# First cross attention on one core: scores of two chunks together, the second score pass on two row halves, key weights folded, tokens rounded on ScalarE

## What is computed

```python
xn = _ln(x, lnx_g, lnx_b)
yn = _ln(y, lny_g, lny_b)            # y: the context, 1500 tokens of 64 features
q = jnp.einsum('bsc,hcd->bhsd', xn, wq)
k = jnp.einsum('btc,hcd->bhtd', yn, wk)
v = jnp.einsum('btc,hcd->bhtd', yn, wv)
a = jax.nn.softmax(jnp.einsum('bhsd,bhtd->bhst', q, k) * D ** (-0.5), axis=-1)
o = jnp.einsum('bhst,bhtd->bhsd', a, v)
```

## Time and profile before

| | |
|---|---|
| median of 3 runs | 628.56 us (625.13 to 633.34) |
| profiled execution | 629.66 us, span 627.8 us, mean granted clock 0.98 |
| busy in the span | PE 566.9 us, PEld 416.1, DVE 444.7, ACT 372.0, POOL 380.6 |
| score matmuls L1143 | first at 115.9 us, last at 304.9 us |
| batch 3 of the first cross attention | 189.98 to 214.50 us |

### The profile page before, as it was taken

How to read it: one execution, slowest core, us unless ns; L and a number is a source line. 1 busy time by engine, 2 the same in 40 slices (tenths; PEclk the granted TensorE clock), 3 DMA queues, 4 the chain that set the end, 5 groups by cost and what they waited for, 6 DMA issues and landing times.

```text
span 627.8 us, 18969 instructions
## 1 busy us (share of the span) xinstructions
PE 566.9 (90%) x8256; PEld 416.1 (66%) x8256; DVE 444.7 (71%) x698; ACT 372.0 (59%) x623; POOL 380.6 (61%) x271
## 2 busy tenths in 40 slices
PE   9788898899999999999888979977889889889897
PEld 4566775566767767666777556664667767778765
DVE  3876728697887887786356774776888988986543
ACT  2335674657657667566462417474677777777552
POOL 1572451488989889864630231175999999977500
PEclk9789999999999999999999999997999999999998
DMA  5830015002101101010013000412422432330000
GB/s 169 238 133 2 3 40 180 2 1 42 34 7 41 26 15 40 3 40 3 2 60 123 2 0 3 99 39 64 103 67 45 96 78 52 78 77 4 2 1 15
DMA packets 33838, 31.81 MB, mean 51 GB/s; under 512 B 27124, under 2 KB 27380, under 8 KB 33756
## 3 DMA queue, kind: packets, MB, share of 16 engines
q1 hardware_dynamic: 33756, 30.60, 18.8%
HBM read 13.06 MB, written 0.23 MB: 21 GB/s over the span
## 4 chain that ended last, share of the span: by engine, by line
PE 62%; DVE 18%; ACT 8%; issue 7%; POOL 3%; DMA 1%; DVEq 0%; POOLq 0%; ACTq 0%
PE psum L1143 9%; DVE scratch L1306 6%; PE psum L1067 5%; PE psum L1119 5%; PE psum L1503 4%; PE psum L1112 4%; PE psum L1114 4%; PE psum L1526 4%; DVE scratch L1291 4%; PE psum L217 3%; POOL scratch L1291 2%; ACT scratch L1276 2%; POOL scratch L652 1%; PE psum L1073 1%; PE psum L248 1%
## 5 line engine op out<-in xcount | busy, mean ns | idle before, releaser
L1291 POOL TENSOR_TENSOR scratch<-scratch 125x896 bf16<-125x896 f32 x143 | 242.7, 1715 | 80.4 <-ACT scratch L1276 79.9
L1306 DVE TENSOR_REDUCE scratch<-psum 128x1 f32<-128x500 f32 x336 | 210.3, 672 | 23.1 <-PE psum L1067 9.6
L1276 ACT ACTIVATE scratch<-psum 125x896 f32<-125x896 f32 x192 | 173.6, 917 | 82.8 <-PE psum L1143 51.1
L1112 PE MATMUL psum<-tok_high,scratch 125*128 125x65 bf16 x1344 | 107.0, 194 | 3.3 <-issue 2.7
L1114 PE MATMUL psum<-tok,scratch 125*128 125x64 bf16 x1344 | 106.4, 194 | 0.0
L1112 PEld LDWEIGHTS psum<-tok_high,scratch 125*128 125x128 bf16 x1344 | 94.8, 98 | 13.9 <-ACT scratch L1276 6.0
L1114 PEld LDWEIGHTS psum<-tok,scratch 125*128 125x128 bf16 x1344 | 88.6, 98 | 17.1 <-issue 0.5
L1143 PE MATMUL psum<-scratch 65*128 65x448 bf16 (+1 forms) x384 | 87.3, 352 | 0.0
L1291 DVE TENSOR_TENSOR scratch<-scratch 125x896 bf16<-125x896 f32 x49 | 67.5, 1383 | 22.8 <-ACT scratch L1276 21.1
L1119 PE MATMUL psum<-tok_high,scratch 125*128 125x65 bf16 x1344 | 72.7, 194 | 4.8 <-POOL scratch L1291 3.1
L1503 PE MATMUL psum<-scratch 128*128 128x500 bf16 x168 | 64.2, 382 | 10.8 <-DVE scratch L1306 6.5
(11 more groups left out here) (340 smaller groups left out, 870.5 us busy)
## 6 DMA issues: line engine op xcount, KB each, us to landing
nrm<-scratch SPq DMA_DIRECT2D x64, 96.0 KB, 2.2
nrm<-w_third SPq DMA_DIRECT2D x32, 96.0 KB, 2.2
raw<-ctx_dram SPq DMA_DIRECT2D x4, 672.0 KB
w_third<-fifth_dram SPq DMA_DIRECT2D x3, 595.0 KB, 6.0
w_third<-third_dram SPq DMA_DIRECT2D x2, 844.0 KB, 8.9
w_third<-third_dram SPq DMA_DIRECT2D x2, 843.5 KB, 6.8
w_fourth<-fourth_dram SPq DMA_DIRECT2D x3, 542.5 KB, 5.8
scratch<-scratch SPq DMA_DIRECT2D x8, 192.0 KB, 2.6
```

The costliest lines, as they stand in the source:

```text
L1112: nc.tensor.matmul(psum[:, sums, 65 * r:65 * r + 65], rows, t1[:, c, :], start=(c == 0 and r == 0), stop=False, skip_group_check=True)
L1276: nc.scalar.activation(CR["p"][0:CP, n % RING, :].rearrange("p (f n) -> p f n", f=2), psum[0:CP, S:S + 2, 0:HALF], ACT.Exp).then_inc(self. ...
L1291: ops.tensor_tensor(CR["pl"][0:CP, n % RING, :], CR["p"][0:CP, n % RING, :], p_high(n % RING), ALU.subtract).then_inc(done, 1)
L1306: nc.vector.tensor_reduce(mxp[:, r, t:t + 1], bank(B, TB), X_AXIS, ALU.max).then_inc(self.aux_freed, 1)
```

## The change

- **Key weights.** `fold_keys_pool`: the first column of a head's key weights is subtracted from the other 63 and from itself. The normalized features of a token add up to zero, so the first feature's term moves into the others and its row is no longer needed. The front waits for this before Q.
- **Second pass.** The first feature's row becomes the row of ones and the shift. `yb` has this row and the 63 others twice, in rows 0 to 63 and 64 to 127; of `qb`, the first half of the columns stands in rows 0 to 63 and the second half in rows 64 to 127. So the two matmuls of the second pass have 64 rows each, in different row halves, and write different banks. The ones are four memsets, the copies into `yb` are two DMAs, and the shift units make 448 columns each (eight matmuls, not seven).
- **Two chunks together.** For even n, `scores_pe` issues the first pass of n and of n+1, then the second pass of n and of n+1; for odd n nothing. The first pass of n+1 waits for the exponential of n-1.
- **Tokens.** GpSimd scales both halves of batch b+2 in chunk 1 and takes the rest in chunk 11; the rounding is done by ScalarE in chunks 4 and 5 (`high_tokens`). Before batch 2, all three steps stay on GpSimd (`split_tokens`).

The core of the diff, with one line of context at most:

```diff
         y_ones = sem("y_ones")
+        ONES = 1.0 + 16256.0 / 2 ** 23
+        def fold_keys_pool(pool):
+            keys = par("a2_wk").rearrange("p (h d) -> p h d", d=65)
+            nc.gpsimd.tensor_copy(keys[:, :, 64:65], keys[:, :, 0:1]).then_inc(key_scaled, 1)
+            pool.wait_ge(key_scaled, 2)
+            nc.gpsimd.tensor_tensor(keys[:, :, 0:64], keys[:, :, 0:64], keys[:, :, 64:65].to_broadcast([128, HEADS, CD]),
+                                    ALU.subtract).then_inc(key_scaled, 1)
+            pool.wait_ge(key_scaled, 3)
             for i in range(2):
-                nc.gpsimd.memset(CR["yb", i][64:65, :], 1.0).then_inc(y_ones, 1)
-                pool.wait_ge(y_ones, i + 1)
+                for k in range(2):
+                    nc.gpsimd.memset(CR["yb", i][64 * k:64 * k + 1, :].bitcast(F32), ONES).then_inc(y_ones, 1)
+                    pool.wait_ge(y_ones, 2 * i + k + 1)
...
                         if b < 3:
-                            pe.wait_ge(y_ones, 2)
+                            pe.wait_ge(y_ones, 4)
                         pe.wait_ge(self.max_set, b + 1)
-                    for r in range(4 * k, min(4 * k + 4, ROWT)):
-                        mm = nc.tensor.matmul(psum[:, B, 128 * (r % 4):128 * (r % 4) + 128],
-                                              nmx[:, r:r + 1].to_broadcast([128, 128]), ident16[:, :],
-                                              start=True, stop=True)
+                    for r in range(3 * k, 3 * k + 4):
+                        lo, hi = max(128 * r, HALF * k), min(128 * r + 128, HALF * k + HALF)
+                        mm = nc.tensor.matmul(psum[:, B, lo - HALF * k:hi - HALF * k],
+                                              nmx[:, r:r + 1].to_broadcast([128, 128]),
+                                              ident16[:, lo - 128 * r:hi - 128 * r], start=True, stop=True)
...
                 pe.wait_ge(act_done.sem, act_done.count("qa"))
-                pe.wait_ge(key_scaled, 1)
+                pe.wait_ge(key_scaled, 3)
...
             def scores_pe(self, pe, n):
-                b, c, i = n // CHUNKS, n % CHUNKS, n // CHUNKS % 2
-                S = 2 + 2 * (n % 2)
-                for lhs, rhs, rows in ((CR["ya", i], CR["qa", i], 128), (CR["yb", i], CR["qb", i], 65)):
-                    if c == 0 and rows != 128:
-                        self.wait_freed(pe, self.index("A", 1, b))
-                        pe.wait_ge(self.yb_in, 16 * (b + 1))
-                        pe.wait_ge(self.front_low, 2)
+                if n % 2:
+                    return
+                b, i = n // CHUNKS, n // CHUNKS % 2
+                chunk = lambda m: slice(128 * (m % CHUNKS), 128 * (m % CHUNKS) + 128)
+                if n == 0:
+                    self.wait_freed(pe, self.index("A", 1, 0))
+                for m in (n, n + 1):
+                    if m >= 2:
+                        pe.wait_ge(self.probs, m - 1)
                     for f in range(2):
-                        mm = nc.tensor.matmul(bank(S + f, HALF), lhs[0:rows, 128 * c:128 * c + 128],
-                                              rhs[0:rows, HALF * f:HALF * f + HALF],
-                                              start=(rows == 128), stop=(rows != 128), skip_group_check=True)
-                return mm
+                        nc.tensor.matmul(bank(2 + 2 * (m % 2) + f, HALF), CR["ya", i][:, chunk(m)],
+                                         CR["qa", i][:, HALF * f:HALF * f + HALF], start=True, stop=False,
+                                         skip_group_check=True)
+                if n % CHUNKS == 0:
+                    self.wait_freed(pe, self.index("A", 1, b))
+                    pe.wait_ge(self.yb_in, 32 * (b + 1))
+                    pe.wait_ge(self.front_low, 2)
+                for m in (n, n + 1):
+                    for f in range(2):
+                        rows = slice(64 * f, 64 * f + 64)
+                        mm = nc.tensor.matmul(bank(2 + 2 * (m % 2) + f, HALF), CR["yb", i][rows, chunk(m)],
+                                              CR["qb", i][rows, HALF * f:HALF * f + HALF], start=False, stop=True,
+                                              skip_group_check=True)
+                        if f:
+                            mm.then_inc(self.scores, 1)
...
                         sums_of_earlier()
-                    if n >= 2:
-                        pe.wait_ge(self.probs, n - 1)
-                    if n < 2:
-                        self.wait_freed(pe, self.index("A", 1, 0))
-                    mm = self.scores_pe(pe, n)
-                    mm.then_inc(self.scores, 1)
+                    self.scores_pe(pe, n)
...
                 if kind == "A":
-                    tile, row = self.shift_row(i)
+                    if b and self is cross1:
+                        self.wait_freed(act, self.index("Q", 1, b))
+                    lo, hi = HALF * k, HALF * k + HALF
+                    tile, row = self.shift_row(i, k)
...
                     self.high_act(act, b + 2, 0)
+                if c in (4, 5) and b < BATCH - 2:
+                    self.high_tokens(act, b + 2, c - 4)
...
                     cols = slice(HALF * k, HALF * k + HALF)
-                    nc.vector.tensor_tensor(CR["qb", i][0:64, cols], bank(B, HALF, 64), CR["qa", i][0:64, cols],
-                                            ALU.subtract).then_inc(self.aux_freed, 1)
+                    nc.vector.tensor_tensor(CR["qb", i][64 * k:64 * k + 64, cols], bank(B, HALF, 64),
+                                            CR["qa", i][0:64, cols], ALU.subtract).then_inc(self.aux_freed, 1)
...
                     projected()
+            def scale_tokens(self, pool, b, k):
+                at = slice(CHUNKS * b + 6 * k, CHUNKS * b + 6 * k + 6)
+                nc.gpsimd.tensor_tensor(nrm[:, at, :], nrm[:, at, :], bc(crstd[:, at], CD), ALU.mult
+                                        ).then_inc(tok_scaled, 1)
                 if self is cross1:
-                    nc.gpsimd.tensor_tensor(src, src, bc(crstd[:, at], CD), ALU.mult).then_inc(tok_scaled, 1)
+                    self.scale_tokens(pool, b, k)
                 nc.gpsimd.tensor_copy(tok[i][:, lot, 64:128], src).then_inc(self.tok_high, 1)
+                self.low_tokens(pool, b, k)
+            def high_tokens(self, act, b, k):
+                at = slice(CHUNKS * b + 6 * k, CHUNKS * b + 6 * k + 6)
+                act.wait_ge(self.pv_done, CHUNKS * (b - 2))
+                if self is cross1:
+                    act.wait_ge(tok_scaled, 2 * b + k + 1)
+                nc.scalar.activation(tok[b % TOKENS][:, 6 * k:6 * k + 6, 64:128], self.src[:, at, :], ACT.Copy
+                                     ).then_inc(self.tok_high, 1)
+            def low_tokens(self, pool, b, k):
+                i, lot = b % TOKENS, slice(6 * k, 6 * k + 6)
                 pool.wait_ge(self.tok_high, 2 * b + k + 1)
-                nc.gpsimd.tensor_tensor(tok[i][:, lot, 0:64], src, tok[i][:, lot, 64:128],
-                                        ALU.subtract).then_inc(self.tok_set, 1)
+                nc.gpsimd.tensor_tensor(tok[i][:, lot, 0:64], self.src[:, CHUNKS * b + 6 * k:CHUNKS * b + 6 * k + 6, :],
+                                        tok[i][:, lot, 64:128], ALU.subtract).then_inc(self.tok_set, 1)
                         self.low_part(pool, nc.gpsimd, n, self.low_pool)
-                    if c in self.split_at and b < BATCH - 2:
-                        if b:
-                            pool.wait_ge(self.pv_done, CHUNKS * b)
-                        if self is cross1 and b == 2:
-                            pool.wait_ge(cx_rstd, 2)
-                        self.split_tokens(pool, b + 2, self.split_at.index(c))
+                    if b < BATCH - 2:
+                        self.tokens_pool(pool, b, c)
+            def tokens_pool(self, pool, b, c):
+                if c == 1:
+                    if b == 2:
+                        pool.wait_ge(cx_rstd, 2)
+                    for k in range(2):
+                        self.scale_tokens(pool, b + 2, k)
+                if c == CHUNKS - 1:
+                    for k in range(2):
+                        self.low_tokens(pool, b + 2, k)
...
                 sp.wait_ge(self.ya_in, 16 * (b + 1))
-                sp.dma_start(CR["yb", b % 2][0:64, :], CR["ya", b % 2][64:128, :]).then_inc(self.yb_in, 16)
+                if b:
+                    sp.wait_ge(self.yb_in, 32 * b)
+                for k in range(2):
+                    sp.dma_start(CR["yb", b % 2][64 * k + 1:64 * k + 64, :], CR["ya", b % 2][65:128, :]
+                                 ).then_inc(self.yb_in, 16)
...
             y_ones_set(pool)
+            fold_keys_pool(pool)
```

26 lines of the change are left out of this document (16 added, 10 removed).

## The result

The changed kernel takes 635.22 us (median of 20 runs, 630.57 to 637.42), the kernel before 630.31 us (median of 20, 624.88 to 633.34), all on the same occasion. The ratio is 1.0077 with a 95% interval of 1.0052 to 1.0102: slower by 4.9 us, between 3.3 and 6.4, well inside 2%. The forecast was 630.5 with a range of 620 to 636.5 and "within 2%" as the likeliest case, so both held, but the step was sized at +2.2 us. Of the 4.7 us between 630.5 and 635.22, 1.8 come from the base: the kernel before has its median at 628.56 in three runs and at 630.31 in twenty. The profiled execution took 636.18 us (span 634.4).

The account below looks back on a forecast made before the run. TensorE was taken as the bound, busy 90% of the span. Seven batches at +0.43 us (+3.0) and the last at -0.8 gave +2.2 us, a median near 630.8; forecast 630.5 us, range 620 to 636.5.

Parts of the forecast that it names:

- parts 1 and 2: Scores of a chunk pair: overlapping row halves save 0.38 us, height changes cost 0.21, giving 1.36 us against 1.52.
- (a): Rival, faster: the drain is cheap for long matmuls, a pair costs 1.15 us, whole near 622.5; chance 15%.
- (b): Rival, slower: row halves do not run beside each other, a pair costs 1.74 us, whole 648; chance 4%.
- part 3: First half of a batch: chunk 5's first pass waits 0.64 us, the output product loses 0.29; net +0.10 us.
- parts 4 and 5: Second half of a batch: steady pairs gain 0.30 us, but 0.97 us stand before the shift rows; net +0.33.
- Rival (c): Forecast waits at chunks 4 and 11 are a third of a microsecond too long each; whole near 626, chance 15%.
- part 6: Work off the path: GpSimd's 1.8 us a batch is worth nothing; key transfers issue far ahead of use.
- Seven batches with next maxima: 7 x 0.43: Seven of the first cross attention's eight batches each grow by 0.43 us, together +3.0 us.
- the forecast case: Whole kernel: the walk through the batches holds, median 627 to 634 us; chance 60%.
- the 6% for trouble of ScalarE at chunks 4 and 5: Case: an exponential queues behind a late cast on ScalarE, TensorE behind it; 634 to 645 us, chance 6%.
- The last ... -0.8 us: Last batch, without next maxima: three pairs give 0.5 us and the end 0.3, so -0.8 us.
- The fold ... in the same group: Front: GpSimd's fold is ready between 88.0 and 90.8 us, before Q at 93.37; without that cover 2.3 us once.

Follow-up runs that it names:

- 1: Changed kernel with scores written chunk by chunk again, row halves and everything else kept; 634.45 us, ratio 1.0061 to the kernel before.
- 6: Changed kernel with each pair ordered first pass, second pass, first pass, second pass, so four changes of height for two; 637.94 us, ratio 1.0137.
- 2: Kernel before with the pairing of chunks alone, second passes still at 65 rows and full width; 638.28 us, ratio 1.0136.
- 4: Changed kernel with pairs only at chunks 0/1, 2/3, 6/7 and 8/9, chunks 4, 5, 10 and 11 single; 629.68 us, ratio 1.0001.
- Experiment 3: Changed kernel with the twelve token casts back on GpSimd at chunks 1 and 11; 634.86 us, ratio 1.0073.
- 10: Kernel before with the fold of the key weights alone added, behind the memsets; 630.26 us, ratio 1.0007.
- 12: Kernel before with one maximum's matmul of each batch moved ahead of the scores of chunk 6; 628.89 us, ratio 0.9982.
- 8: Changed kernel with pairs only at chunks 0/1, 2/3, 6/7, 8/9, the context's last statistics moved and the fold ahead of the memsets; 630.84 us, ratio 1.0009.
- experiment 9: As experiment 8, plus one maximum's matmul of each batch moved ahead of the scores of chunks 6 and 7; 627.64 us, ratio 0.9976 to the kernel before.

## Why the prediction was right, and where it was off

- **Overlap of the row halves and the price of a drain (parts 1 and 2): right.** A pair takes 1.34 us for the forecast 1.36, a change of height 0.10 to 0.11 (experiments 1 and 6). Rivals (a) and (b) are both out.
- **The wait at chunk 4 (part 3): right.** 0.66 us for 0.64, the output product 0.28 late (206.12 for 205.84) for 0.29, the first half of the batch 11.78 for 11.78.
- **Steady pairs and the wait at chunk 11 (parts 4 and 5): right.** Shift rows 4.02 behind their pair for 4.04, second half 13.16 for 13.17. Rival (c), waits a third of a microsecond too long, is out. Experiments 2 and 4 price the waits by edits: 1.34 us on the kernel before, 0.62 on the changed one against no pair at the tight places.
- **Casts, key transfers (part 6): right for seven batches.** Experiment 3 changes a steady batch by nothing. GpSimd's busy time fell by 0.86 us in batch 3 (21.74 to 20.88) and not by 1.8; it did not matter.
- **"Seven batches with next maxima: 7 x 0.43": a step that failed.** I took batch 3 for all. Five were as it, the second was +0.27, and the first was +1.37, because VectorE's sum of the context (1.74 us) stands in it where the pairs have no slack. This row was in the trace of before. It is a term of the sum that was missing, +0.9 (the second batch gives 0.2 back). The measured 635.22 lies above the forecast case (627 to 634) and in the band of the 6% for trouble of ScalarE at chunks 4 and 5 (634 to 645), but that trouble did not come: the square there cost nothing.
- **"The last ... -0.8 us": right to the last exponential (-1.05 from the batch's first exponential, -0.75 from its first scores), wrong as a term of the sum.** TensorE's last sums wait for the low parts and are only 0.48 earlier, and then the clock goes to 1.2 GHz for 3 to 4 us and takes 1.0. The sum ended at the last exponential instead of at the next thing that waits.
- **"The fold ... in the same group" ready in time: right, and still not free.** TensorE never waited for it, but VectorE did: 0.2 us. I had priced the wait of its consumer only.
- **Ahead of the first exponential: two terms put at nothing.** The first pair brings its exponential 0.3 us later, which the sum has nowhere, and the shift rows of the front cost 0.1.

To the +2.2 forecast come 0.9 for the first batch, -0.2 for the second, 0.3 for what the last one gives back, 1.0 for the clock and 0.6 for what lies ahead of the first exponential. That makes +4.8, against 4.9 measured (3.3 to 6.4). So each wait inside a steady batch was sized right, and more than half of the step lies outside the five steady batches, where the sum had copied batch 3 or had no term.

**What stays open.** What decides whether the clock falls behind the cross attention: TensorE's work there is the same, it falls in 10 of 14 traces there and in one elsewhere, and it stayed up in before, 1 and 10, which have neither pairs nor a moved maximum. TensorE stands a little longer in the low parts of the changed kernel (busy 5.07 of the 6 us ahead of the thin stretch, 5.54 in the kernel before), but this does not decide it: 4 and 12 with 5.60 and 5.54 fall, 8 with 5.60 does not. It was not tried to fill the stretch with matmuls. And the times less the distance to the second cross attention scatter by 5 us between kernels (333.0 to 338.5), 333.0 to 335.5 with the old front and 333.9 to 338.5 with the new; the traces find 0.6 us of that ahead of the first exponential. Much of the scatter goes with the clock. Within one kernel the executions with a lower mean granted clock are the longer ones, by about 3.9 us for each 0.01 (an estimate, a line fitted through the 243 executions of all kernels, each against its own kernel's mean; it takes up half of the scatter). The executions of experiments 8 and 1 had mean clocks of 0.976 and 0.977, those of the other kernels 0.978 to 0.983. Put at 0.980 by that line, the mean times are 628.8 for experiment 8 and 632.4 for 1, against 630.2 to 630.8 for the kernel before on four occasions, 634.6 for the changed one and 627.4 for experiment 9. This fits what theory A said of both; whether these two kernels have a lower clock of their own or had it by chance, twelve executions each do not tell.

## What to carry to other kernels

Doing two steps together takes away the work that lay between them, and that work was covering waits: list what each second step waits for, and pair only where it is already there (here the waits took 1.34 us a batch, the row halves gave 0.92 back, and leaving out two of six pairs was worth 0.62). Walk through the first and the last pass of a loop as well as a steady one, and end the sum at the next consumer, not at the last instruction of the loop. An operation that is hidden on its own engine can still hold another one.

## What was not expected of the hardware

- A VectorE scaling of 128x112 values took 0.28 us beside an idle GpSimd and 0.58 or 0.87 beside a busy one, a memset as much as a subtraction, and ended about when GpSimd did; the instruction of VectorE ahead of it ran beside the same fold at its usual 0.33 us.
- With the same work of TensorE ahead of it (2.32 of 4 us busy), the granted clock fell to 0.65 of full speed over the next 4 us in one kernel and stayed at 1.00 in the other; the four f32 matmuls there spanned 1.70 us against 1.04.
- The first exponential of the cross attention came between 113.61 and 120.03 us in traces of nearly the same front. The three earliest (experiments 8, 9 and 1) had a mean granted clock of 0.94, 0.89 and 0.89 from 20 to 50 us, the others 0.72 to 0.83.
